# A recommendation tower on one core: four more split product pairs a chunk, new first loads, gathers spread over the steps

## What is computed

```python
for i in range(3):
    z = (x0[:, :, None, :] * h[:, None, :, :]).reshape(B, F * G, E)
    y = relu(einsum('oc,bce->boe', Ws[i], z) + bs[i][None, :, None])
    x_keep, h = (y[:, :half], y[:, half:]) if i != 2 else (y, y)
    xs.append(x_keep)
z = sum(concatenate(xs, axis=1), axis=2)
h = maximum(concatenate([z, dense_ctx], axis=1) @ W_top1 + b_top1, 0)
h = maximum(h @ W_top2 + b_top2, 0)
return h @ W_top3
```

## Time and profile before

| | |
|---|---|
| median of 3 runs | 634.18 us (634.15 to 635.11) |
| the profiled execution | 636.44 us, its span 633.4 us |
| mean granted clock of TensorE | 0.920 |
| busy share of the span | PE 85%, DVE 57%, POOL 30%, ACT 22% |
| x_pair loads by L275 | 120 of 512 KB, 6.8 us from issue to landing (median) |

### The profile page before, as it was taken

The page is one execution under the profiler, slowest core; times in us unless marked ns, Lnnn a source line. Parts: engine busy times, 40 slices in busy tenths (PEclk is TensorE's granted clock), DMA queues, the critical chain, the costliest instruction groups (busy, mean ns, idle before and its releaser), DMA issues.

```text
span 633.4 us, 3860 instructions
## 1 busy us (share of the span) xinstructions
PE 538.8 (85%) x1350; PEld 260.6 (41%) x1350; DVE 358.9 (57%) x212; ACT 136.4 (22%) x194; POOL 191.9 (30%) x162
## 2 busy tenths in 40 slices
PE   3804312479799999999999999999999999999998
PEld 3301100135345454545454544545454545454446
DVE  1201110176494949585767768594949494948531
ACT  1110000033312231313131314040413222220303
POOL 5760000044643435251616070707162020200000
PEclk9666656579899999999999999999999999999999
DMA  4341116939587879797979697879697877550200
GB/s 132 48 133 50 50 50 150 206 93 247 149 215 147 216 166 228 146 229 153 221 151 231 147 230 153 220 158 223 151 217 158 208 186 163 132 132 4 69 0 0
DMA packets 35170, 94.45 MB, mean 149 GB/s; under 512 B 7937, under 2 KB 15105, under 8 KB 27217
## 3 DMA queue, kind: packets, MB, share of 16 engines
q1 hardware_dynamic: 27984, 91.47, 60.2%
q0 software_dynamic: 4096, 1.06, 1.9%
q10 hardware_dynamic: 3072, 1.70, 1.0%
HBM read 92.04 MB, written 2.10 MB: 149 GB/s over the span
## 4 chain that ended last, share of the span: by engine, by line
PE 78%; SPq 12%; DMA 5%; ACT 1%; DVE 1%; POOL 1%; issue 1%; DVEq 0%
PE acc L567 69%; SPq L285 11%; PE acc L578 6%; DMA x_pair<-x_scratch 4%; POOL gathered L317 1%; DVE z L385 1%; PE acc L588 1%; PE acc L583 1%; ACT h L479 0%; DMA gathered<-in_table,rows_all 0%; DMA row<-in_row 0%; DMA x_scratch<-gathered 0%; PE acc L653 0%; PE h L653 0%; PE h L588 0%
## 5 line engine op out<-in xcount | busy, mean ns | idle before, releaser
L567 PE MATMUL acc<-z,w_direct 128*128 128x512 f32 x1024 | 459.1, 609 | 79.7 <-DVE z L385 74.3
L567 PEld LDWEIGHTS acc<-z,w_direct 128*128 128x128 f32 x1024 | 199.5, 196 | 330.1 <-issue 262.2
L385 DVE TENSOR_TENSOR z<-h,x_pair 128x2048 f32<-128x2048 f32 (+1 forms) x65 | 145.0, 2252 | 213.6 <-ACT h L479 129.5
L330 POOL TENSOR_TENSOR z_low<-z,z_high 128x1024 fp32r<-128x1024 f32 x30 | 70.2, 2362 | 320.4 <-ACT z_high L465 320.4
L317 POOL DMA_INDIRECT gathered<-in_table,rows_all x128 | 121.5, 949 | 40.5 <-issue 35.4
L385 DVE TENSOR_TENSOR z<-h_odd,x_pair 128x2048 f32<-128x2048 f32 x32 | 72.4, 2283 | 8.9 <-ACT h_odd L479 8.8
L385 DVE TENSOR_TENSOR z<-h_even,x_pair 128x2048 f32<-128x2048 f32 x32 | 72.2, 2281 | 8.0 <-ACT h_even L479 8.0
L479 ACT ACTIVATE h<-acc,columns 64x512 f32<-64x512 f32 x32 | 20.8, 652 | 224.4 <-PE acc L578 213.9
L465 ACT ACTIVATE z_high<-z 128x1024 fp32r<-128x1024 f32 x30 | 30.1, 1049 | 73.9 <-DVE z L370 73.9
L479 ACT ACTIVATE kept<-acc,columns 64x512 f32<-64x512 f32 (+1 forms) x48 | 32.8, 683 | 54.6 <-PE acc L567 53.8
L370 DVE TENSOR_TENSOR z<-x_rep,x_rot 128x2048 f32<-128x2048 f32 x15 | 34.2, 2281 | 0.0
(11 more groups left out here) (119 smaller groups left out, 121.7 us busy)
## 6 DMA issues: line engine op xcount, KB each, us to landing
x_pair<-x_scratch SPq DMA_DIRECT2D x120, 512.0 KB, 6.8
x_rot<-x_scratch SPq DMA_DIRECT2D x56, 256.0 KB, 5.2
x_pair<-x_scratch SPq DMA_DIRECT2D x16, 256.0 KB
x_rep<-x_scratch SPq DMA_DIRECT2D x14, 256.0 KB, 5.0
w_direct<-in_W SPq DMA_DIRECT2D x2, 1024.0 KB, 17.0
gathered<-in_table,rows_all POOLq DMA_INDIRECT x128, 6.0
x_scratch<-gathered SPq DMA_DIRECT2D x30, 64.0 KB, 9.4
x_rot<-x_scratch ACTq DMA_DIRECT2D x4, 256.0 KB, 4.5
```

The costliest lines, as they stand in the source:

```text
L330: nc.gpsimd.tensor_tensor(z_low[:, slot_of(pair)], products_of(pair), z_high[:, slot_of(pair)].bitcast(F32), ALU.subtract).then_inc(low_po ...
L385: nc.vector.tensor_tensor(z[:, step.group % Z_SLOTS, first:end], h[:].unsqueeze(1).to_broadcast([P, end - first, N]), x_pair[:, chunk % 2, ...
L567: op = nc.tensor.matmul(acc[pair.layer][:], w_direct[:, first + i], products_of(pair)[:, i], start=i == 0 and pair is OPENS[pair.layer, pa ...
```

## The change

- `hands` splits four more pairs of each chunk from 1 on: (1, k=0, second pair), (1, k=1, second), (2, k=1, second), (2, k=2, second). `AT` gives the place of each pair's weights in `w_high` and `w_low`, which grow from 4 to 12 tiles; ACT and DVE split those weights at the start. The split matmuls go into `acc[pair.layer]`.
- `x_pair` of chunk 0 is loaded by `load_pair`, and W2 right after W1.
- The eight gathers of a chunk are issued one a step, from step (1,c-3,0) on.
- 64 transposes at the start instead of 40.
- The top layers: `wt2_high` and `wt2_low` lie in `w_high` and `w_low` and wait for the last split pair that uses these (LAST1); the four products with the dense inputs come first; the second relu of hid2 is on DVE; the output is two matmuls of 512 columns into one partition, copied and stored as one row.

```diff
-BUSY = 40
+BUSY = 64
-def hands(layer, chunk):
-    return ("pool", "pool") if layer == 0 and chunk else ("tensor", "tensor")
+SPLIT = ((1, 0, 1), (1, 1, 1), (2, 1, 1), (2, 2, 1))
+AT = {(0, 0, 0): 0, (0, 0, 1): 2} | {of: GROUP + 2 * n for n, of in enumerate(SPLIT)}
+def hands(layer, chunk, k):
+    return tuple("pool" if chunk and (layer, k, i) in AT else "tensor" for i in range(2))
...
-            sp.dma_start(flat(w_direct[:, 0:TILES]), w12_in[0]).then_inc(w12_here[0], 16)
+            for layer in range(2):
+                sp.dma_start(flat(w_direct[:, layer * TILES:(layer + 1) * TILES]), w12_in[layer]).then_inc(
+                    w12_here[layer], 16)
...
-            sp.wait_ge(x_stored[0], 32)
-            x = x_dram[0]
-            for t in range(TILES):
-                both = bass.AP(x.tensor, x.offset + t * N, [[ROT * N, 2], [0, HALF], [1, N]])
-                sp.dma_start(x_pair[:, 0, t, :], both).then_inc(first_pair_here[t // GROUP], 16)
-            sp.dma_start(flat(w_direct[:, TILES:2 * TILES]), w12_in[1]).then_inc(w12_here[1], 16)
-            for k in range(GROUPS):
-                load_pair(1, k)
+            for c in range(2):
+                for k in range(GROUPS):
+                    load_pair(c, k)
...
-                ahead = step.chunk + AHEAD
-                if step.layer == 1 and step.k == 0 and ahead < CHUNKS:
-                    if ahead >= X_SLOTS:
-                        before = ahead - X_SLOTS
-                        pool.wait_ge(x_stored[before % 2], 32 * (before // 2 + 1))
-                        if before == 0:
-                            pool.wait_ge(first_here, 16)
-                    for j in range(GATHERS):
-                        gather(ahead, j)
+                for c in range(AHEAD, CHUNKS):
+                    j = n - PLACE[1, c - AHEAD, 0]
+                    if 0 <= j < GATHERS:
+                        if j == 0 and c >= X_SLOTS:
+                            before = c - X_SLOTS
+                            pool.wait_ge(x_stored[before % 2], 32 * (before // 2 + 1))
+                            if before == 0:
+                                pool.wait_ge(first_here, 16)
+                        gather(c, j)
...
+            for n, of in enumerate(SPLIT):
+                dve.wait_ge(w_rounded, 3 + n)
+                nc.vector.tensor_tensor(flat(w_low[:, AT[of]:AT[of] + 2]), flat(weights_of(*of)),
+                                        flat(w_high[:, AT[of]:AT[of] + 2]).bitcast(F32),
+                                        ALU.subtract).then_inc(w_ready, 1)
...
+            dve.wait_ge(top2_done, 2)
+            nc.vector.tensor_scalar(out=hid2[:, 1, :], in0=acc[1][:], scalar1=bt2[:, 1:2], scalar2=0.0,
+                                    op0=ALU.add, op1=ALU.max).then_inc(hid2_dve, 1)
             dve.wait_ge(top3_done, 1)
-            nc.vector.tensor_copy(result[:], out_bank[0][:, 0:BATCH // P]).then_inc(half_result, 1)
-            dve.wait_ge(half_result, 1)
-            nc.vector.tensor_tensor(result[:], out_bank[1][:, 0:BATCH // P], result[:],
-                                    ALU.add).then_inc(result_ready, 1)
+            nc.vector.tensor_copy(result[:], out_bank[0:1, :]).then_inc(result_ready, 1)
...
+            for layer, k, i in SPLIT:
+                at = AT[layer, k, i]
+                act.wait_ge(w12_here[layer - 1], 16)
+                nc.scalar.activation(flat(w_high[:, at:at + 2]), flat(weights_of(layer, k, i)),
+                                     ACT.Copy).then_inc(w_rounded, 1)
...
-                        op = nc.tensor.matmul(acc[0][:], w[:, 2 * pair.i + i], zs[:, slot, i],
+                        op = nc.tensor.matmul(acc[pair.layer][:], w[:, at + i], zs[:, slot, i],
...
+            pe.wait_ge(hid2_act, 1)
+            nc.tensor.matmul(out_bank[0:1, :], wt3[:, 0:1], hid2[:, 0, :], start=True, stop=False)
+            pe.wait_ge(hid2_dve, 1)
+            nc.tensor.matmul(out_bank[0:1, :], wt3[:, 1:2], hid2[:, 1, :], start=False, stop=True).then_inc(top3_done, 1)
```

More of the change, by code:

```diff
@@ L80, in step @@
         pairs = []
-        for i, by in enumerate(hands(layer, chunk)):
+        for i, by in enumerate(hands(layer, chunk, k)):
             pairs.append(Pair(layer, chunk, k, i, counts["group"], by, counts[by], counts["split"]))
@@ L117 @@
 assert not BEHIND[len(PLAN)] and not BEHIND[len(PLAN) + 1]
+LAST1 = max((pair for step in PLAN for pair in step.by("pool") if step.layer < 2), key=lambda pair: pair.split)
+assert AT[SPLIT[1]] + 2 == 2 * N // P and SPLIT[1][0] == 1
 def flat(tiles):
@@ L195, in dlrm_tower @@
         wd = x_pair[0:COPIES * EMBED, 0, 10, :]
+        wt2_high, wt2_low = [flat(w[:, 0:2 * N // P]) for w in (w_high, w_low)]
         sum01_high, sum01_low = zl_high[:], zl_parts[:]
@@ L220, in dlrm_tower @@
         x_stored = [sem("x_stored_even"), sem("x_stored_odd")]
-        first_pair_here = [sem(f"first_pair_here_{k}") for k in range(GROUPS)]
         xp_here = [[sem(f"xp_here_{b}_{k}") for k in range(GROUPS)] for b in range(2)]
@@ L242, in products_of, with weights_of @@
             return z[:, pair.group % Z_SLOTS, 2 * pair.i:2 * pair.i + 2]
+        def weights_of(layer, k, i):
+            first = TILES * (layer - 1) + GROUP * k + 2 * i
+            return w_direct[:, first:first + 2]
         def wait_made(eng, step):
@@ L325, in _ @@
                     gather(c, j)
-            for step in PLAN:
+            for n, step in enumerate(PLAN):
                 for pair in step.by("pool"):
@@ L532, in _ @@
             act.wait_ge(top_here, 16 * TOPS)
-            for high, full in ((wd_high, wd), (wt1_high, wt1), (wt2_high, wt2)):
-                nc.scalar.activation(high[:], full, ACT.Copy).then_inc(top_rounded, 1)
+            for high, full in ((wd_high[:], wd), (wt1_high[:], wt1), (wt2_high, wt2)):
+                if high is wt2_high:
+                    act.wait_ge(pairs_used, LAST1.split + 1)
+                nc.scalar.activation(high, full, ACT.Copy).then_inc(top_rounded, 1)
             act.wait_ge(sum01_made, CHUNKS)
@@ L546, in _ @@
                 nc.scalar.activation(hid1_high[:, m, :], hid1[:, m, :], ACT.Copy).then_inc(hid1_rounded, 1)
-            for m in range(2):
-                act.wait_ge(top2_done, m + 1)
-                nc.scalar.activation(hid2[:, m, :], acc[m][:], ACT.Relu, bias=bt2[:, m:m + 1]).then_inc(hid2_ready, 1)
+            act.wait_ge(top2_done, 1)
+            nc.scalar.activation(hid2[:, 0, :], acc[0][:], ACT.Relu, bias=bt2[:, 0:1]).then_inc(hid2_act, 1)
         @block.tensor
@@ L573, in split @@
                 open_bank(pair)
-                slot = slot_of(pair)
+                slot, at = slot_of(pair), AT[pair.layer, pair.k, pair.i]
                 pe.wait_ge(low_dve if pair.by == "vector" else low_pool, pair.count + 1)
@@ L630, in _ @@
             for m in range(4):
-                cols = slice(m * P, (m + 1) * P)
-                nc.tensor.matmul(top_bank[m][:], wd_parts[:, cols], dense_parts[:], start=True, stop=False)
-                three_products(top_bank[m], (wt1_high[:, 0], wt1_low[:, 0]), cols, (sum01_high, sum01_low),
-                               False, False)
+                nc.tensor.matmul(top_bank[m][:], wd_parts[:, m * P:(m + 1) * P], dense_parts[:], start=True, stop=False)
+            for m in range(4):
+                three_products(top_bank[m], (wt1_high[:, 0], wt1_low[:, 0]), slice(m * P, (m + 1) * P),
+                               (sum01_high, sum01_low), False, False)
             pe.wait_ge(sum_split, 1)
@@ L647, in _ @@
                         op.then_inc(top2_done, 1)
-            for k in range(2):
-                pe.wait_ge(hid2_ready, k + 1)
-                for m in range(4):
-                    rows = hid2[:, k, :].rearrange("p (b m) -> p m b", m=4)[:, m, :]
-                    op = nc.tensor.matmul(out_bank[k][:, m:m + 1], rows, wt3[:, k:k + 1], start=True, stop=True)
-            op.then_inc(top3_done, 1)
+            pe.wait_ge(hid2_act, 1)
+            nc.tensor.matmul(out_bank[0:1, :], wt3[:, 0:1], hid2[:, 0, :], start=True, stop=False)
+            pe.wait_ge(hid2_dve, 1)
+            nc.tensor.matmul(out_bank[0:1, :], wt3[:, 1:2], hid2[:, 1, :], start=False, stop=True).then_inc(top3_done, 1)
 def kernel(**inputs):
```

30 lines of the change are left out of this document (13 added, 17 removed).

## The result

The changed kernel takes **589.15 us** (median of 4 runs, 588.97 to 590.67), the kernel before beside it 634.64 (634.15 to 635.15): a ratio of 0.929, 95% interval 0.927 to 0.931. The forecast of 541 us was wrong, and so was its range: 589 lies 23 us above the upper end. The sign was right, and half of the expected gain came.

The account below looks back on a forecast made before the run. Bound taken: PE in the steady stretch, transfers at the start. From 636.44 us, -79.4 - 0.7 + 1.9 - 10.6 - 1.7 - 3.1 = -93.6 gives 542.8, or 541 us as the median of runs; range 531 to 566.

Parts of the forecast that it names:

- From there nothing is new up to T(1): At the start, after chunk 0's layer 1: the old stretch of 20.2 us was taken over unchanged.
- T(1): Time at which PE ends chunk 1's layer-0 products: forecast 67.5 us, 79.4 earlier than before.
- Chunk 0's layer 1: At the start: PE ends it at 47.3 us, including 3.0 us for a clock drop after a 2.7 us gap.
- rival 2: At the start, the clock falls all the same: 51.8 us instead of 47.3, total 545 us; chance 0.20.
- T(1) to T(2): From the end of chunk 1's layer-0 products to chunk 2's: two of eight pairs are split, -0.7 us.
- The turn: Steady stretch, one chunk each: period 29.03 us plus 0.5 of ACT waits, 29.55, so -0.88 each and -10.6 over twelve.
- low d: A low part on POOL in the steady stretch: runs 15.7 to 18.1 us into it, 0.15 us to spare for PE.
- Rival 1: Steady stretch: DVE and POOL hinder each other, periods of 31.0 to 31.9 us, total 558 to 569 us; chance 0.30.
- S and U: PE time for a pair of tiles: 1.366 us split and 1.717 us unsplit, 0.351 us saved.
- Rival 3: Steady stretch: no ACT stall, twelve periods of 29.03 us, total 534 us; chance 0.08.
- rival 4: The start's loads don't get as fast, a group each 10.2 us: T(1) 20 us later, total 561 us; chance 0.05.
- rival 5: POOL sets the period: slower than before from x (low part time) = 4.45 us, 645 us at x = 4.8; chance 0.02.

Follow-up runs that it names:

- r2: The changed kernel with SyncE issuing chunk 1's x_pair loads only after chunk 1's x_rep and x_rot have landed: 576.86 us.
- e7: The changed kernel with 40 transposes at the start instead of 64: 594.23 us.
- e4: The changed kernel without the four further split pairs, layers 1 and 2 all unsplit: 573.88 us.
- e1b: The changed kernel with DVE's layer-0 product reading x_rep from PSUM and, from chunk 4, the square part its square: 569.4 us.
- r6: The changed kernel with replica and squares in PSUM, one ACT rounding behind the next relus, chunk 1's x_rep and x_rot ahead of its x_pair: 553.49 us.
- e1a: The changed kernel with only the layer-0 product reading x_rep from PSUM, copied there by ACT: 578.97 us.
- e3: The changed kernel with ACT rounding pair (1,c,0,1) behind the relus of the next step: 566.9 us.

## Why the prediction was wrong, step by step

- **"From there nothing is new up to T(1)"** is the step that failed first, +19.7 us. The 20.2 us were taken from a trace in which x_rep and x_rot of chunk 1 had landed by 49.8 us, 77 us before the copied stretch begins. There L285 was slow and chunk 1's x_pair loads stood behind it. Now ACT's store (issued at 32.1 us) lands at 42.56, behind the last of chunk 0's 4 MB (41.75), and its landing lets go both ACT's 1.25 MB of x_rep and x_rot and SP's 4 MB of chunk 1's x_pair, which land together at 69.2. The estimate priced what the faster transfer brings, and not what it collides with. The Trainium skill, DMA: Bandwidth & Descriptors (Issuing engines are not separate DMA queues), says that transfers started by different engines run on the same 16 DMA engines and interleave. r2 agrees: with SP's loads held back the x_rot load on ACT's queue takes 4.20 us against 23.93.
- **Chunk 0's layer 1** ended at 47.8, against 47.3 forecast, by errors that cancel: the relu came at 29.65 and not at 26.8, and the last x_pair landed at about 41.8, not 38.4, for 209 to 217 GB/s were moved from 22 to 28 us and not 266; but PE ran at the full clock from 30 to 48 us, so the 3.0 us for a cold clock were not spent. Of rival 2 this much is right: the granted clock fell at 24 us (0.62 and 0.53 to 28 us) instead of at 20, and chunk 0's layer 0 took 5.6 us (23.98 to 29.61) for the 3.7 of the sum. The other 0.9 of T(0)'s 2.85 us is a later start: the spread matmuls began at 19.50, not 18.6. All of it was hidden by the loads. Whether the transposes as such count for the clock no run tells, since e7's start was held up.
- **T(1) to T(2)**, +5.0: e4 gives 21.3, so the split pairs cost 4.3 where they were to save 0.7. The exclusion is 1.9 of it (e1b 23.75); the rest wasn't taken apart.
- **The turn** is the other step that failed, +21.8 us: "0.15 to spare" for low d, with a gather at 0.94 us and DVE's layer-0 work at its old length. The prediction had seen that DVE and POOL might exclude one another and gave it 0.30. It was so. Rival 1 put low d's end at 19.7 us after T if the square part goes first, and the turn at 31.0; measured 19.73 and 31.30. That the end fits to 0.03 us is partly luck, for the way was another: the gather, which the sum let pass in 0.94 us, is the one that is held, and low d follows it at its own pace. The order of ACT was rightly seen and its size nearly (0.72 us, e1b against r6, for 0.5), and S and U too: a turn with no wait is 29.09, for 29.03.
- Rival 3 (no stall, 534 us) and rival 4 were wrong as put; the 20 us at T(1) that rival 4 had came, by another cause. In rival 5 the sum at x = 4.8 doesn't come out: 13 turns of 2.1 us on top of 634 are 661 us, not 645.
- **Turn 2, the end and the tail** came within 0.5 us each, T(15) to the end 64.9 for 64.7, and by the mechanism that was named: PE waited 7.45 us for chunk 1's kept relu in turn 2, for 7.5.

The chance of rival 1 was too low for a rule with no row against it. The Trainium skill, SBUF — State Buffer (Who interferes with whom), states that a DVE instruction with two SBUF inputs and a GpSimd one that reads SBUF block each other for a whole instruction. The trace agrees in both directions: with the low part first, the square part takes 2.13 us against 0.74 in e1a and the product 3.10 against 2.28 in e3; with the DVE instruction first, a low part takes 3.99 and 2.83 us against 2.4 (the rows of the turn without gathers above). The same section reports that a DVE tensor_tensor did not stall a DMA of POOL's queue; here one on two SBUF tensors held an indirect gather, 2.83 us against 0.94, and the measurement decides. The range erred by taking each rival alone: both the late T(1) and the exclusion came, and no case had the two.

## What to carry to other kernels

When a slow transfer is made fast, list what it was keeping apart: everything issued behind it comes forward, and a small load on another queue whose data somebody waits for can then land 20 us late. Put such loads first, and take every wait that the slow transfer had hidden as not priced yet: T(1) hung on one. When POOL gets work beside DVE, give DVE's long instructions one operand in PSUM, and look through the written order of the engine in between for a step that stands ahead of what two others wait for.

## What the runs showed of the hardware

- An indirect gather issued by POOL is held by DVE instructions on two SBUF tensors, to 0.17 us behind the end of the last: 2.83 us against 0.94. So are POOL's low parts and, if POOL was first, the DVE instructions. With one DVE operand in PSUM both run at full speed side by side (e1b: 0.96 and 2.28 us).
- A 64 KB store takes 1.6 us from issue to landing at the median of the changed kernel, and 10.05 us on ACT's queue and 16.91 on SP's when 4 MB of x_pair loads were issued before it; a 256 KB load takes 4.2 us without them and 23.9 beside them.
- The hold-up: engines that pass work to each other at intervals of 2 to 4 us, or not at all for 30, while the first 4 MB of loads run, in some sittings and not in others, with the same program. The kernel before took 633.6 to 634.7 us at the median of every sitting: there the loads of L285 set T(1), whatever the start did; the last is issued at 91.75 us and landed at 117.87 (the chain of before). The cause of the hold-up is open.

```profile
91.75 26.12 DMA x_pair<-x_scratch
```
